# Attention and mixer of a graph network on one Trainium2 core: the place of the score sums, of the message sums and of half of the mixer

## The reference, cut to what matters

```
# attention over edges (H = 8 heads of 32)
score = einsum('ehd,ehd->eh', q[edge_dst], k[edge_src]) / sqrt(32)
ex    = exp(clip(score, -10, 10))            # softmax over the edges of a node
wv    = segment_sum(ex * v[edge_src], edge_dst) / segment_sum(ex, edge_dst)

# mixer over the same 3125 nodes
h   = relu(batchnorm(x @ w_qkv))             # 256 -> 768 channels
s   = grouped 32x32 products of (h * w_dw)   # joined to h: 1536 channels, 16 groups
out = relu(q) * relu(k).sum * v / v.sum      # per group of 32, with a norm per node
fx  = tanh-like squash of (out @ w_res) + b_res
```

## Time and profile before

| what | us |
|---|---|
| median of three runs | 3358.8 |
| the profiled execution, its own time | 3332.88 |
| its span | 3331.1 |
| the `ab` phase's loop in it, roughly 1595 to 2465 | 870 |
| DVE busy in that stretch | 684.71 |
| PE busy in that stretch | 662.87 |

### The profile page before, as it was taken

One profiled execution on the slowest core, in us unless ns is written; L12 is line 12 of the kernel. 1 busy time (PEld: TensorE's weight loads), 2 busy tenths in 40 slices (PEclk: granted clock), 3 DMA queues, 4 the chain that ended last, 5 costly groups with the idle time before them and its releaser, 6 DMA issues. The chain is left out here.

```text
span 3331.1 us, 62976 instructions
## 1 busy us (share of the span) xinstructions
PE 2531.7 (76%) x17412; PEld 2046.0 (61%) x17412; DVE 2124.7 (64%) x4254; ACT 1258.8 (38%) x2585; POOL 1249.2 (38%) x971
## 2 busy tenths in 40 slices
PE   5547555777569999775678777877756966999997
PEld 5435344666457777552556566666545855899986
DVE  7655454653558888855468788788866556444455
ACT  1432211411145555433444545444334343454442
POOL 0058786688500000000666566656633002211125
PEclk9668855888759999887889999988876976999998
DMA  5338674233200000015765656556553004566633
GB/s 138 93 81 210 166 203 128 66 83 84 57 20 10 19 19 9 19 62 165 169 162 150 156 152 157 159 140 164 142 146 83 0 0 168 170 236 236 223 124 88
DMA packets 251663, 387.61 MB, mean 116 GB/s; under 512 B 117456, under 2 KB 175661, under 8 KB 246878
## 3 DMA queue, kind: packets, MB, share of 16 engines
q0 software_dynamic: 151392, 170.67, 21.0%
q1 hardware_dynamic: 87224, 202.62, 19.2%
q10 hardware_dynamic: 12864, 12.06, 1.2%
HBM read 323.76 MB, written 60.56 MB: 115 GB/s over the span
## 5 line engine op out<-in xcount | busy, mean ns | idle before, releaser
L922 POOL DMA_INDIRECT ms_got<-gather,edge_src x400 | 524.2, 1311 | 165.2 <-issue 119.0
L2128 POOL DMA_INDIRECT ab_gkv<-gather_kv,edge_src x200 | 268.8, 1344 | 171.3 <-PE ab_total L2304 109.6
L2128 POOL DMA_INDIRECT xz_rows<-gather_kv,edge_src x205 | 272.2, 1328 | 160.5 <-PE ab_total L2304 105.4
L970 PE MATMUL ms_total<-ms_got,ms_hot 125*125 125x256 f16 x1040 | 181.4, 341 | 167.4 <-DVE ms_hot L943 122.7
L970 PEld LDWEIGHTS ms_total<-ms_got,ms_hot 125*125 x1040 | 154.1, 175 | 201.9 <-issue 201.3
L1636 ACT ACTIVATE ex_h<-ex_up,ex_now 128x313 f32<-128x313 f32 (+1 forms) x320 | 195.9, 612 | 198.0 <-PE ex_up L701 190.8
L3045 DVE CAST moe_hidden<-moe_h 128x256 f16<-128x256 f32 (+1 forms) x336 | 100.5, 299 | 200.0 <-ACT moe_h L2982 200.0
L1852 POOL MEMSET br_one<- 125x1 f16 x1 | 0.1, 107 | 604.3 <-POOLq L126 604.3
L2982 ACT ACTIVATE moe_h<-moe_up,wring 128x256 f32<-128x256 f32 (+1 forms) x336 | 163.2, 486 | 125.0 <-PE moe_up L701 83.6
L2287 PE MATMUL ab_picked<-y_rows,xz_rows 125*125 x1060 | 176.1, 327 | 32.2 <-issue 21.6
L2287 PEld LDWEIGHTS ab_picked<-y_rows,xz_rows 125*125 x1060 | 147.8, 163 | 66.5 <-issue 64.5
(11 more groups left out here) (527 smaller groups left out, 6003.8 us busy)
## 6 DMA issues: line engine op xcount, KB each, us to landing
wring<-wsplit SPq DMA_DIRECT2D x33, 2052.0 KB
ab_dsts<-in_dst SPq DMA_DIRECT2D x83, 305.2 KB
wsplit<-mix_split SPq DMA_DIRECT2D x32, 512.0 KB, 5.0
mix_raw<-in_L_ffn_W1p SPq DMA_DIRECT2D x16, 512.0 KB, 7.5
mix_raw<-in_L_ffn_W2p SPq DMA_DIRECT2D x16, 512.0 KB, 9.9
results<-moe_made SPq DMA_DIRECT2D x32, 256.0 KB, 7.5
ms_got<-gather,edge_src POOLq DMA_INDIRECT x400, 4.2
gather_kv<-qkv_out SPq DMA_DIRECT2D x5, 1120.0 KB
```

What stands on the lines that cost most here:

```text
L922: pool.indirect_dma_start(out=self.got[:, s, j, :], out_offset=None, in_=self.m.gather0, in_offset=bass.IndirectOffsetOnAxis(ap=self.m.edg ...
L970: ins = pe.matmul(self.total[:, visit % 2, 0:C], self.hot[:, visit % RING, j, :], self.got[:, s, j, p * C:(p + 1) * C], start=(j + p == 0) ...
L2128: pool.indirect_dma_start(out=gkv[s][:, j, 0:2 * C], out_offset=None, in_=m.gather_kv, in_offset=bass.IndirectOffsetOnAxis(ap=m.edge_src[: ...
```

## The change

ACT's part is split like PE's: half of the CONV or JOIN units of a step are read ahead of `weights(n+1)` and half behind it, and OUT's copy and its squares go behind it too. PE makes the totals `sums(n)` ahead of the second half of the mixer's part. DVE sums the scores of group n+1 ahead of the one-hots of group n, and clips them behind these; a new semaphore `reduced` orders the clip behind the sum, in place of the chained wait.

```
 ACT
-                def part(c, s):
+                def part(c, s, late):
                     if s in CONV:
-                        for u in range(4 * s, 4 * s + 4):
+                        for u in range(4 * s + 2 * late, 4 * s + 2 * late + 2):
                             convolved(c, u)
                     if s in JOIN:
-                        for k in range(4):
+                        for k in range(2 * late, 2 * late + 2):
                             joined(c, JOIN.index(s), k)
+                    if s in OUT and late:
+                        (wait for s_ot, copy to o_cols, squares: as before)
+                    if late:
+                        return
...
                 for n in range(G):
                     for c, s in chunks_at(n):
-                        part(c, s)
+                        part(c, s, False)
                     bounds = group_bounds(act, m, n + 3)
                     weights(n + 1, (n + 1) % GATHERED)
+                    for c, s in chunks_at(n):
+                        part(c, s, True)
                     one_hots(n + 3, (n + 3) // 2, (n + 3) % 2, bounds)
 PE
                     pick_q(n + 2, ahead)
+                    sums(n, n % GATHERED, bounds)
                     for c, s in chunks_at(n):
                         part(c, s, True)
-                    sums(n, n % GATHERED, bounds)
 DVE
                 def scores(g):
                     dve.wait_ge(s_qk, g + 1)
-                    v.link(dve.tensor_reduce(score, qk, ALU.add))
+                    dve.tensor_reduce(score, qk, ALU.add).then_inc(s_reduced, 1)
+
+                def clip(g):
+                    dve.wait_ge(s_reduced, g + 1)
                     dve.tensor_scalar(score, 10.0, -10.0, ALU.min, ALU.max).then_inc(s_score, 1)
...
                     multiply(n + 1)
                     weigh(n)
+                    scores(n + 1)
                     bounds = group_bounds(dve, m, n)
                     visits(n, n, bounds)
-                    scores(n + 1)
+                    clip(n + 1)
                     for c, s in chunks_at(n):
                         late(c, s)
```

More of the change, by code:

```diff
@@ L2102, in attention_and_ball @@
         s_apart, s_pick, s_pickv, s_picked, s_qk = (ph.sem(x) for x in ("apart", "pick", "pickv", "picked", "qk"))
-        s_score, s_exp, s_spread = (ph.sem(x) for x in ("score", "exp", "spread"))
+        s_score, s_exp, s_spread, s_reduced = (ph.sem(x) for x in ("score", "exp", "spread", "reduced"))
         s_hot, s_total, s_added, s_pace, s_v = (ph.sem(x) for x in ("hot", "total", "added", "pace", "v"))
@@ L2216, in joined, with part @@
                     act.activation(cat[:, j, 2, k * 4:k * 4 + 4, :], parts[:, 2, :, :], ACT.Copy).then_inc(s_read, 1)
-                def part(c, s):
+                def part(c, s, late):
                     if s in CONV:
-                        for u in range(4 * s, 4 * s + 4):
+                        for u in range(4 * s + 2 * late, 4 * s + 2 * late + 2):
                             convolved(c, u)
                     if s in JOIN:
-                        for k in range(4):
+                        for k in range(2 * late, 2 * late + 2):
                             joined(c, JOIN.index(s), k)
+                    if s in OUT and late:
+                        j = OUT.index(s)
+                        t = c * J + j
+                        act.wait_ge(s_ot, t + 1)
+                        act.activation(o_cols[:, :, :].rearrange("p b r -> p (b r)"), o_bank[:, 0:CO // 128 * R],
+                                       ACT.Copy).then_inc(s_oc, 1)
+                        turned[c] = squared(cat[:, j, 0, :, :].rearrange("p g d -> p (g d)"), s2[:, 4, j:j + 1])
+                    if late:
+                        return
                     if s == WEIGH[0]:
@@ L2235, in part @@
                         act.activation(fx[:, j, :], o_bank[0:R, 0:C], ACT.Copy).then_inc(s_raw, 1)
[L2236 to L2242, removed]
                     if s == ROOTS:
@@ L2384, in scores, with clip @@
                     dve.wait_ge(s_qk, g + 1)
-                    v.link(dve.tensor_reduce(score[:, :], qk[:, :].rearrange("p (k d) -> p k d", d=HD), AX_X, ALU.add))
+                    dve.tensor_reduce(score[:, :], qk[:, :].rearrange("p (k d) -> p k d", d=HD), AX_X, ALU.add)\
+                        .then_inc(s_reduced, 1)
+                def clip(g):
+                    dve.wait_ge(s_reduced, g + 1)
                     dve.tensor_scalar(score[:, :], score[:, :], 10.0, -10.0, ALU.min, ALU.max).then_inc(s_score, 1)
@@ L2471, in _ @@
                 scores(0)
+                clip(0)
                 adder = Adder(nc, dve, "ab", summed, total, s_total, s_added, lag=LATE, ring=LATE)
```

## The result

The changed kernel takes 3404.6 us (median; 3395.1 to 3407.6), the kernel before 3358.8 (3351.6 to 3361.9). The ratio is 1.0145, 95% interval 1.0118 to 1.0171: slower by 46 us. The forecast was +29 us, 3388 us, with a range of its own of +12 to +50. The same kernel, measured again on another chip for the last experiment, took 3395.1 us against 3337.2 there, 58 us more by the medians and 55 by the ratio of 1.0164.

What follows compares the result with a forecast made beforehand. DVE's line was taken as the loop's time, with the ring setting the period after the change. Four periods +26 us, steps 0 to 12 +6, steps 64 to 79 -3: 3358.8 + 29 = 3388 us, range 3371 to 3409.

Steps and rivals of the forecast that it cites:

- The ring: PE's picks, totals, second half, ACT's reading, ACT's one-hots, PE's next picks: 9.6 us a JOIN step, 8.6 with OUT.
- (3): ACT's second half behind the exponential: wins 0, but closes a loop through PE and ACT once around each step.
- Its sum: Nine turns, steps 28 to 37: 82.7 us of steps, 12.2 for second-visit totals, 6.3 for second-visit picks, together 101.2.
- The third rival: The ring is longer and binds everywhere, PE's clock being lower: +64 us, 3423 us, chance 0.18.
- (2): PE's totals ahead of its second half: DVE's 24 stalls before a second `hot` fall from 112.5 to 72 us.
- hand-worked period: Steps 28 to 38, followed link by link: 112.9 us between multiplication starts, 105.9 before, so 7.0 later.
- the ceiling: Most that (1) and (2) could win on DVE's stalls: 40 us, about 8 in each of five periods' worth of steps.
- (4): DVE's `early` at s = 12 waits for ACT's last JOIN read, now behind the totals: 2.9 us later, five times.
- (1): DVE's score sum ahead of the one-hots: `hot` done 4.0 us behind the multiplication, not 2.53; DVE's work unchanged.
- +6: Steps 0 to 12, without mixer work on DVE: 6 us slower, taken between bounds of -5 and +20.
- -3: Steps 64 to 79, without a CONV or JOIN half: 3 us faster, from the stalls alone.
- The first rival: DVE's gaps alone decide: 40 us won, 2.9 lost five times at `early`, -25 us, 3334 us, chance 0.20.

Runs made afterwards that it cites:

- the last experiment: Ballast added to the changed kernel (3443.6 us against 3395.1) and to the kernel before (3335.4 against 3337.2), all measured on one chip.
- Cutting it at PE's end: Changed kernel with PE's order as before, second half ahead of totals: 3312.4 us against 3343.8 for the kernel before, ratio 0.9898.
- at ACT's: Changed kernel with ACT making the one-hots of group n+3 ahead of its second half: 3338.5 us against 3343.8 for the kernel before, ratio 0.9987.
- ballast: One more squared sum on ACT ahead of each step's one-hots: changed kernel 3443.6 us against 3395.1, kernel before 3335.4 against 3337.2.

## Why the prediction was right, and what was mis-sized

**The ring, (3): right, shown.** Its mark, PE waiting for ACT's one-hots, is there. Cutting it at PE's end (-31 us) or at ACT's (no difference to before) takes the loss away, and ballast on it costs where the ring was said to bind and hardly anywhere else. Its terms hold in the steps of one visit: a JOIN step was priced 9.6 us and steps 29 and 33 took 9.26 and 9.27 (picks' end to picks' end), with totals of 3.00 us in them in place of 2.48; an OUT step was priced 8.6 and steps 30 and 34 took 8.34 both. The price left out about 0.5 us from the one-hots' end to the picks (2035.05 to 2035.55 above), and the other links are shorter than their rows of before by more than that. DVE's waits for picks, 42.9 us for a forecast of about 40, lie elsewhere than forecast: 27 of them in the first twelve steps, and only 18, with two that stand under "issue", ahead of the multiplications that open the steps of p = 11.

**Its sum: the mis-sized term.** From the picks' end of step 28 to that of step 37 I had 101.2 us; it took 108.9, 1929.17 to 2038.07. Nearly all of the excess sits in the steps with a second visit or an extra pair of picks. Step 35, and the granted clock (last but two) in the stretch of each total:

```profile
2011.10 0.28 PE L2295 MATMUL ab_picked<-y_rows,ab_zeros 125*125 125x1 f16 x3
...
2011.85 4.13 PE L2308 MATMUL ab_total<-ab_gkv,ab_hot 125*125 125x264 f32 x10 [0.47 <-issue]
2017.54 2.48 PE L2308 MATMUL ab_total<-ab_gkv,ab_hot 125*125 125x264 f32 x10 [1.56 <-DVE ab_hot L2411]
...
2011.85:2016.00 4.15, 4.13 (x10) 2.91 (x10) 0.00 (x0) 0.00 (x0) 2.07 (x2) 0.59 0.76 198
...
2017.50:2020.00 2.50, 2.46 (x12) 2.12 (x13) 1.85 (x3) 0.00 (x0) 0.00 (x0) 1.00 0.09 32
```

The first total takes 4.13 us where the same ten matmuls take 2.48 below it, and in the turn shown further above the picks take 2.30, not 1.34. I priced every matmul at 2.4 GHz, and took the lower clock into the stalls alone. On the ring the engines take turns, and PE stands still once or twice a step: the granted clock of steps 25 to 37 is 0.91, where it was 0.95 before and is 0.94 with the ring cut, at PE's end or at ACT's. The third rival named this: 0.5 us in each of nine steps, 11 us a period. The slow groups of matmuls in these nine turns take 11 us more than the same groups at full clock (totals 7.3, picks 3.0, the rest 0.8), which covers the excess of 7.7; the links that came shorter than priced give the difference. The largest single turn, step 28 to 29, took 20.3 us where the price is 15.8, with both totals slow (4.17 and 3.73 us) and the second picks too (2.34). The four periods of 13 steps came out longer by 9.6, 14.0, 12.0 and 9.8 us where I had 6.6 for each.

**The totals in front, (2): wrong in the changed kernel.** I had the 24 stalls fall to 72 us, "70 to 90" among the marks. They rose to 125.2. The 2.76 us a stall holds only where PE is on time; behind the ring it lags. In step 35 the second `hot` waited 7.30 us: the 2.76 priced, 1.65 for the slow total, and 2.9 of lag:

```profile
2007.72 0.86 DVE L2411 SCALAR_TENSOR_TENSOR ab_hot<-row_no,ab_node,edge_dst 125x625 f32<-125x625 f32 x1
...
2016.22 0.87 DVE L2411 SCALAR_TENSOR_TENSOR ab_hot<-row_no,ab_node,edge_dst 125x625 f32<-125x625 f32 x1 [7.30 <-PE ab_total L2308]
```

The hand-worked period has three such steps on the ring (28, 31 and 35), and yet I gave the ceiling as the win on DVE's line. The gain asked for no totals in front at all: with PE's old order and the other two parts most of it is there, 81.2 us of stalls.

**`early`, (4): right in kind, a third too small.** 39.7 us in five times, forecast 35 or more. In step 38 its multiplication started 120.7 us behind step 28's (2044.41 less 1923.67), forecast 112.9; nearly all of the difference is the ring's 7.7. Its own cost, priced at 2.9 us a time, is 4.2 with the ring cut (29.3 less 8.2, by five).

**Scores in front, (1): the gain is real, 22 us alone.** Of it 12 us are the stalls' and some 10 to 13 the shorter steps that I had at nothing, with 7 lost again to gathers; the profiled loops differ by 17 us, and the rest is not accounted for.

**Steps 0 to 12 and 64 to 79.** +6 was taken for the first stretch and +10.1 came. Picks ended four of DVE's long waits there (7.9, 4.3, 7.5 and 7.2 us) and the waits for gathers shrank, but the ring is not shown to be the reason: with the ring cut at ACT's end the stretch is 12 us longer than before, and the ballast on the ring adds nothing to it. What sets it stays open. -3 was taken for the last, +0.2 came.

**The number.** The profiled loop is 55 us longer than before where the sum said 29: 45 in the four periods for 26, 10 for 6, 0 for -3. The mechanism was right and every one of these terms came out higher. That the first medians give +46, inside the range of +12 to +50, is partly luck; the second measurement gives +58.

**The first rival,** the gaps of DVE alone, is what the Trainium skill's page "Perfetto Trace Analysis", section "Optimization Strategy", says to go by: make start sooner what the most-contended engine waits for. The trace agreed on the engine and the gap. PE's move is made for this gap. Alone it did shrink the gap, from 112.5 to 98.9 us, and the kernel still lost 88 us, in other waits; in the whole change the gap grew by 12.7 us, since what moved back was on the way to the next picks, and behind late picks the totals are late too.

## What to carry to other kernels

Ahead of moving an instruction on one engine, follow what it pushes back through the other engines until it returns to its own queue; add once around, and compare with the step of the engine that sets the time. A ring shows in no busy share: all engines had slack here, and 0.61 us a step on one that was 45% busy cost 10 to 13 us in each period of 13 steps that the ring bound. Ballast on an idle engine, in both versions, is a cheap way to find it. And don't price a ring's matmuls all at full clock: here PE stopped in each turn, and its slow groups cost 11 us in nine turns.

## What was not expected of the hardware

The same ten total matmuls took 4.13 and 2.48 us within one step. PE had waited 2.3 us for one-hots, ran the picks behind this wait at full speed (1.34 us) and was slow in the total after them: granted clock 0.59 there, 1.00 in the second total, so near the lower of the two levels, 1.2 GHz, and then at the upper, 2.4 GHz. PE's mean clock over the span hides this (0.865, before 0.859); only the stretch's own value shows it.
